# Gate products of a token stage as three-part fp32r products, with the parts made by GpSimd, ScalarE and VectorE

## What is computed

```python
out_swa = _swa(x_in, wq, wk, wv, wo)                # windowed attention
upd = ...                                           # one gradient step on a two-layer MLP (w1, b1, w2, b2)
out_mem = _mlp(*upd, k_flat)                        # silu(x @ w1.T + b1) @ w2.T + b2 with the updated weights
g1 = jax.nn.sigmoid(out_swa @ lin1.T)
g2 = jax.nn.sigmoid(out_mem @ lin2.T)
out_merged = g1 * out_swa + g2 * out_mem
...
x = x + ga * out_merged
h = _layernorm(x) * (1 + cb) + sb                   # input of router, shared expert and routed experts
```

## Time and profile before

| | |
|---|---|
| median of three runs | 1879.82 us |
| profiled execution | 1880.22 us, its span 1878.5 us |
| TensorE busy | 1827.2 us (97%) |
| VectorE, ScalarE, GpSimd busy | 1230.8, 955.1, 946.2 us |
| stage 2, 755 to 1213 us: TensorE, VectorE, ScalarE, GpSimd busy | 452.6, 327.1, 217.8, 248.4 of 458 us |
| granted TensorE clock in each stage | 0.99 |

### The profile page before, as it was taken

The page is one execution under the profiler, slowest core; times in us unless marked ns, Lnnn a source line. Parts: engine busy times, 40 slices in busy tenths (PEclk is TensorE's granted clock), DMA queues, the critical chain, the costliest instruction groups (busy, mean ns, idle before and its releaser), DMA issues.

```text
span 1878.5 us, 36384 instructions
## 1 busy us (share of the span) xinstructions
PE 1827.2 (97%) x12428; PEld 1607.6 (86%) x12428; DVE 1230.8 (66%) x2454; ACT 955.1 (51%) x1789; POOL 946.2 (50%) x667
## 2 busy tenths in 40 slices
PE   7999999999999999999999999998999999999995
PEld 5888888888888888677788877898999999999994
DVE  8877777777777777566776668744555555555552
ACT  6656666666666665545453354333344444444341
POOL 5666566666666665025666656644323333323234
PEclk9999999999999999999999999999999999999998
DMA  6211111111111100302111012267889888898883
GB/s 228 68 38 38 34 34 37 34 35 36 37 34 46 43 31 21 130 20 69 46 47 46 16 30 63 69 207 233 289 280 289 290 286 263 289 290 285 285 281 85
DMA packets 141016, 234.08 MB, mean 125 GB/s; under 512 B 24756, under 2 KB 88971, under 8 KB 140816
## 3 DMA queue, kind: packets, MB, share of 16 engines
q1 hardware_dynamic: 116368, 220.50, 34.3%
q0 software_dynamic: 24576, 12.69, 4.6%
HBM read 194.58 MB, written 78.45 MB: 145 GB/s over the span
## 4 chain that ended last, share of the span: by engine, by line
PE 53%; DMA 3%; issue 2%; POOL 1%; DVE 1%; SPq 0%; ACT 0%; POOLq 0%; DVEq 0%; ACTq 0%
PE bank L85 26%; PE bank L1904 21%; PE bank L1169 4%; DMA out_rows<-c_y_rest,c_token_rest 2%; DMA c_w<-in_e1T 1%; PE bank L2126 1%; POOL out_rows L2078 1%; PE bank L1668 1%; POOL slots L1863 0%; DMA slots<-last_row,last_index 0%; PE bank L2137 0%; DVE b_h_low L1450 0%; SPq L1960 0%; DVE early L1547 0%; DVE c_y_rest L2045 0%
## 5 line engine op out<-in xcount | busy, mean ns | idle before, releaser
L1904 PE MATMUL bank<-c_xT,c_w 128*128 128x160 f32 x3072 | 431.1, 300 | 5.7 <-DMA c_w<-in_e1T 5.0
L1904 PEld LDWEIGHTS bank<-c_xT,c_w 128*128 128x128 f32 x3072 | 420.5, 190 | 7.1 <-DMA c_w<-in_e1T 6.0
L1863 POOL DMA_INDIRECT slots<-b_row,b_index x224 | 249.1, 1112 | 199.1 <-issue 117.9
L2078 POOL DMA_INDIRECT out_rows<-c_y,c_x x64 | 100.2, 1565 | 374.0 <-DMA out_rows<-c_y_rest,c_token_rest 220.2
L2026 DVE TENSOR_TENSOR c_gT<-bank,c_sil 128x480 f32<-128x480 f32 x128 | 84.2, 658 | 218.8 <-PE bank L1904 209.8
L1994 ACT CAST c_gTs_high<-c_gT 128x384 fp32r<-128x384 f32 x128 | 65.6, 513 | 137.5 <-DVE c_gT L2026 121.2
L1987 ACT ACTIVATE c_sil<-bank 128x480 f32<-128x480 f32 x128 | 73.0, 570 | 113.0 <-PE bank L1904 100.9
L2019 DVE TENSOR_TENSOR c_gTs_low<-c_gT,c_gTs_high 128x384 fp32r<-128x384 f32 x128 | 71.7, 560 | 74.6 <-ACT c_gTs_high L1994 64.1
L456 POOL TENSOR_TENSOR last_row<-last_row,a_e 128x256 f32<-128x256 f32 x33 | 54.4, 1649 | 125.7 <-DVE a_e L712 124.1
L85 PE MATMUL bank<-c_w2s_high,c_gTs_high 128*128 128x256 f32 x384 | 114.2, 297 | 0.9 <-DVE c_gTs_low L2019 0.9
L85 PE MATMUL bank<-c_w2s_high,c_gTs_low 128*128 128x256 f32 x384 | 107.1, 279 | 0.0
(11 more groups left out here) (329 smaller groups left out, 5455.4 us busy)
## 6 DMA issues: line engine op xcount, KB each, us to landing
c_w<-in_e1T SPq DMA_DIRECT2D x64, 1536.0 KB
c_w<-in_e2T SPq DMA_DIRECT2D x48, 768.0 KB
early<-in_e2T SPq DMA_DIRECT2D x16, 768.0 KB
slots<-a_fill SPq DMA_DIRECT2D x16, 642.0 KB
c_x<-slots SPq DMA_DIRECT2D x64, 160.5 KB
a_x_in<-in_x SPq DMA_DIRECT2D x32, 128.0 KB, 2.1
xT_tiles<-a_xT SPq DMA_DIRECT2D x32, 128.0 KB
swaT_tiles<-a_swaT SPq DMA_DIRECT2D x32, 128.0 KB
```

The costliest lines, as they stand in the source:

```text
L1863: pool.indirect_dma_start(out=T["slots"], out_offset=bass.IndirectOffsetOnAxis(ap=index[:, t, k:k + 1], axis=0), in_=row[:, t, :], in_offs ...
L1904: return nc.tensor.matmul(out, lhsT, rhs, start=first, stop=last, skip_group_check=True)
L2078: pool.indirect_dma_start(out=T["out"], out_offset=bass.IndirectOffsetOnAxis(ap=token, axis=0), in_=rows, in_offset=None, bounds_check=las ...
```

## The change

In stage 2 both gate products become split products. linT is held as two parts, linT_high and linT_low; it is loaded into the place of x2 as the first load of the stage, GpSimd rounds the high part and VectorE makes the low part. For each chunk GpSimd rounds swaT to high_swaT and subtracts to get low_swaT (`split_swaT`): for chunks 0 and 1 at the start of its program, for chunk c+1 at group k=4 of the scatters of `routed_chunk(c)`, before the pace wait of that group. For om, ScalarE rounds high_om (`om_high`, between the sigmoids of the two gates) and VectorE makes low_om right after each om block. TensorE waits for `swaT_low` and, by k, for `om_high` and `om_low`.

The new buffers take addresses of others: low_swaT that of om, high_swaT that of g1, high_om that of g2, low_om that of hm; `fits` is `rest`. So `split_swaT` waits for the turning of the merged rows (`mT_mm`), `om_high` waits for `mT_mm` and `base_out`, and the sigmoid of g1 waits for both gate products of attention.

```diff
-        sp.dma_start(linT[:], T["linT"]).then_inc(S("lin_in"), 16)
+        sp.dma_start(lin_raw, T["linT"].rearrange("p a k d -> p (a k d)")).then_inc(S("lin_in"), 16)
+        load_swaT(0)
         for cols, raw in s1_raw:
             sp.dma_start(raw, T["s1T"].rearrange("p k n -> p (k n)")[:, cols]).then_inc(S("s1_in"), 16)
...
+        def split_swaT(c):
+            wait_apart(pool, S("swaT_in"), 16 * (c + 1), S("passed_pool"))
+            if not isinstance(c, int) or c > 0:
+                wait_apart(pool, S("mT_mm"), 2 * c, S("passed_pool"))
+            pool.tensor_copy(flat(high_swaT[:]), flat(swaT[:])).then_inc(S("swaT_high"), 1)
+            wait_apart(pool, S("swaT_high"), c + 1, S("passed_pool"))
+            pool.tensor_tensor(flat(low_swaT[:]), flat(swaT[:]), flat(high_swaT[:]).bitcast(F32), ALU.subtract).then_inc(S("swaT_low"), 1)
+
         def pace(c, k):
+            if k == 4:
+                split_swaT(c + 1)
...
+        pool.wait_ge(S("lin_in"), 16)
+        pool.tensor_copy(flat(linT[0][:]), lin_raw).then_inc(S("lin_high"), 1)
+        split_swaT(0)
+        pool.wait_ge(S("s1_low"), len(s1_raw))
+        split_swaT(1)
         routed_chunk(1, 1, pace)
...
+        def om_high(c):
+            wait_past(act, S("mT_mm"), 2 * c)
+            wait_past(act, S("base_out"), (c - 1) * 16)
+            for m in range(DC):
+                act.wait_ge(S("om"), 2 * c + m + 1)
+                act.copy(block_of(high_om, m), block_of(om, m)).then_inc(S("om_high"), 1)
...
             for g, (dst, banks) in enumerate(((g1, (5, 6)), (g2, LIN2_BANK if after else LIN2_FIRST))):
+                if g == 1:
+                    om_high(c)
                 for m in range(DC):
-                    act.wait_ge(S("lin_mm"), c * 4 + 2 * g + m + 1)
+                    act.wait_ge(S("lin_mm"), c * 4 + 2 * g + (m + 1 if g else DC))
...
                    .then_inc(S("om"), 1)
+                dve.wait_ge(S("om_high"), 2 * c + m + 1)
+                low(block_of(low_om, m), block_of(om, m), block_of(high_om, m)).then_inc(S("om_low"), 1)
...
         clamps()
+        dve.wait_ge(S("lin_high"), 1)
+        low(flat(linT[1][:]), lin_raw, flat(linT[0][:])).then_inc(S("lin_low"), 1)
...
         def gate_of_attention(c, m):
             for k in range(DC):
-                ins = mm(bank(5 + m), linT[:, 0, k, m * P:(m + 1) * P], block_of(swaT, k), k == 0, k == DC - 1)
+                ins = mm_split(nc, bank(5 + m), cut(linT, slice(None), 0, k, slice(m * P, (m + 1) * P)),
+                               [block_of(a, k) for a in swaTs], k == 0, k == DC - 1)
...
+        def gate_of_memory(c, banks):
+            for k in range(DC):
+                pe.wait_ge(S("om_high"), 2 * c + k + 1)
+                for a, part in enumerate((0, 1)):
+                    for m in range(DC):
+                        mm(bank(banks[m]), linT[part][:, 1, k, m * P:(m + 1) * P], block_of(high_om, k),
+                           k == 0 and a == 0, False)
+                pe.wait_ge(S("om_low"), 2 * c + k + 1)
+                for m in range(DC):
+                    ins = mm(bank(banks[m]), linT[0][:, 1, k, m * P:(m + 1) * P], block_of(low_om, k),
+                             False, k == DC - 1)
...
-                pe.wait_ge(S("lin_in"), 16)
-            pe.wait_ge(S("swaT_in"), 16 * (c + 1))
+                pe.wait_ge(S("lin_low"), 1)
+            pe.wait_ge(S("swaT_low"), c + 1)
```

More of the change, by code:

```diff
@@ L1115, in token_stage @@
     w1T, w2T, mod, ident, b1c, b2c = (buf[k] for k in ("w1T", "w2T", "mod", "ident", "b1c", "b2c"))
-    linT = sb("linT", [P, 2, DC, D])
+    linT_high = sb("linT_high", [P, 2, DC, D], F32R)
     wgT = sb("wgT", [P, DC, E])
@@ L1132, in token_stage @@
     hidden = buf["early"][:].rearrange("p (j n) -> p j n", j=HC)
-    om = sb("om", [P, TPC, D])
-    g1 = sb("g1", [P, TPC, D])
-    g2 = sb("g2", [P, TPC, D])
+    with ExitStack() as plain:
+        om, g1, g2 = (plain.enter_context(nc.sbuf_tensor("b_" + name, [P, TPC, D], F32)) for name in ("om", "g1", "g2"))
+    low_swaT, high_swaT, high_om = (sb(name, [P, TPC, D], F32R) for name in ("low_swaT", "high_swaT", "high_om"))
     x = sb("x", [P, TPC, D])
     x2 = sb("x2", [P, TPC, D])
-    hm = sb("hm", [P, TPC, D])
+    with ExitStack() as plain:
+        hm = plain.enter_context(nc.sbuf_tensor("b_hm", [P, TPC, D], F32))
+    low_om = sb("low_om", [P, TPC, D], F32R)
     hT = sb("hT", [P, DC, CH])
@@ L1147, in token_stage @@
     rank = sb("rank", [P, TPC, E])
-    fits = sb("fits", [P, TPC, E])
+    fits = rest
     slot = sb("slot", [P, TPC, E])
@@ L1163, in token_stage @@
     row = [sb(f"row{p}", [P, TPC, ROW]) for p in range(2)]
+    sb("low_shift", [P, SHIFT // 12])
+    linT = (linT_high, sb("linT_low", [P, 2, DC, D], F32R))
+    lin_raw = x2[:].rearrange("p t d -> p (t d)")
+    swaTs, oms = (high_swaT, low_swaT), (high_om, low_om)
     def bank(b, n=CH):
@@ L1234, in store @@
             sp.dma_start(out_rows[:, tiles(c - 1), :], base[:]).then_inc(S("base_out"), 16)
+        sp.dma_start(lin_raw, T["linT"].rearrange("p a k d -> p (a k d)")).then_inc(S("lin_in"), 16)
+        load_swaT(0)
         for cols, raw in s1_raw:
             sp.dma_start(raw, T["s1T"].rearrange("p k n -> p (k n)")[:, cols]).then_inc(S("s1_in"), 16)
-        load_swaT(0)
-        sp.dma_start(linT[:], T["linT"]).then_inc(S("lin_in"), 16)
         sp.dma_start(wgT[:], T["wgT"]).then_inc(S("wg_in"), 16)
@@ L1299, in gpsimd @@
         last_slot = pool.to_reg(E * CAP - 1)
-        pool.wait_ge(S("s1_low"), len(s1_raw))
+        pool.wait_ge(S("lin_in"), 16)
+        pool.tensor_copy(flat(linT[0][:]), lin_raw).then_inc(S("lin_high"), 1)
         def routed_chunk(c, p, step):
@@ L1390, in body @@
             for g, (dst, banks) in enumerate(((g1, (5, 6)), (g2, LIN2_BANK if after else LIN2_FIRST))):
+                if g == 1:
+                    om_high(c)
                 for m in range(DC):
-                    act.wait_ge(S("lin_mm"), c * 4 + 2 * g + m + 1)
-                    wait_past(act, S("mT_mm"), 2 * c)
-                    if g == 1:
-                        wait_past(act, S("base_out"), (c - 1) * 16)
+                    act.wait_ge(S("lin_mm"), c * 4 + 2 * g + (m + 1 if g else DC))
                     act.activation(block_of(dst, m), by_tile(bank(banks[m])), ACT.Sigmoid)\
@@ L1762, in gate_of_attention @@
             for k in range(DC):
-                ins = mm(bank(5 + m), linT[:, 0, k, m * P:(m + 1) * P], block_of(swaT, k), k == 0, k == DC - 1)
+                ins = mm_split(nc, bank(5 + m), cut(linT, slice(None), 0, k, slice(m * P, (m + 1) * P)),
+                               [block_of(a, k) for a in swaTs], k == 0, k == DC - 1)
             ins.then_inc(S("lin_mm"), 1)
+        def gate_of_memory(c, banks):
[9 more added lines that the diff above has]
+                             False, k == DC - 1)
+                    if k == DC - 1:
+                        ins.then_inc(S("lin_mm"), 1)
         def hidden_layer(c, after, js):
@@ L1806, in body @@
                 ranks(c)
-            for k in range(DC):
-                pe.wait_ge(S("om"), 2 * c + k + 1)
-                for m in range(DC):
-                    ins = mm(bank((LIN2_BANK if after else LIN2_FIRST)[m]), linT[:, 1, k, m * P:(m + 1) * P], block_of(om, k), k == 0, k == DC - 1)
-                    if k == DC - 1:
-                        ins.then_inc(S("lin_mm"), 1)
+            gate_of_memory(c, LIN2_BANK if after else LIN2_FIRST)
             if after and not last:
```

## The result

The changed kernel takes 1908.13 us (median of 6 runs, 1898.06 to 1913.91), the kernel before, beside it, 1880.28 (1879.34 to 1886.24). The ratio is 1.014, with a 95% interval of 1.0116 to 1.0164: slower, as predicted, but by 28 us at the medians where +7.6 was predicted, and outside the range of 1882.0 to 1892.5. The profiled execution is the shortest of the six: 1898.06 us, with a span of 1896.3 against 1878.5 before. So the trace can account for 17.8 us of the difference, and not for the 28 us between the medians.

What follows compares the result with a forecast made beforehand. TensorE was taken as the bound, only 0.88 us ahead of the hm chain; -0.5 us up to the end of chunk 1 and +8.1 for six chunks gave +7.6, so 1887.4 us, range 1882.0 to 1892.5.

Steps and rivals of the forecast that it cites:

- The hold: Chunks 2 to 7: GpSimd's copy and subtraction of swaT block VectorE's 128x4 inverse-root steps, delaying hm by 3.2 us.
- rivals 1 and 2: Inverse-root steps in stage 2: 1, no hold reaches them, -10.4 us, chance 0.14; 2, only the subtraction holds, +2.8 us, 0.08.
- rival 3: GpSimd's swaT copy takes its upper bound of 1.75 us: hm delayed 3.9 us, +11.8 us in all, chance 0.10.
- rival 4: Main case plus the om chain 0.4 us late in each chunk: +3.2 us, 1890.6 us, chance 0.06.
- The sum: Each of six chunk boundaries: hm turned 2.38 us later, 1.035 gained after it, +1.35 us a chunk, +8.1 in all.
- Chunks 0 and 1: Start of stage 2 to the end of chunk 1: gain less a shorter hold at boundary 0 to 1, -0.5 us.
- The gain of 1.1 in chunk 0: Chunk 0's four gate product pairs, less the om wait, bring its last gate product and merge about 1.1 us earlier.
- The om side: Memory gate in each chunk: om's high and low parts arrive just in time, cost zero, at most 0.4 us a chunk.
- Stage 3 "shifts as a whole": Stage 3 starts by TensorE's end of stage 2 and moves with it, adding no gain or loss.

Runs made afterwards that it cites:

- experiment 7: Changed kernel with GpSimd's copy and subtraction of swaT one scatter earlier (k=3, not k=4): median 1882.86 us, ratio 1.0017 to the kernel before.
- experiment 5: Changed kernel with TensorE computing one attention gate product twice more where it waited for hm: median 1892.89 us, ratio 1.0075 to the kernel before.
- experiment 2: Kernel before, fp32 products kept, plus GpSimd's rounding copy and subtraction into dead buffers at k=4 of six chunks: median 1904.67 us, ratio 1.014.
- experiment 12: Kernel before with three more 128x1024 subtractions on VectorE ahead of the inverse root at six boundaries: median 1910.66 us, ratio 1.0159.
- experiment 1: The changed kernel run again, nothing altered: median 1904.99 us, ratio 1.0163 to the kernel before.
- experiment 3: Changed kernel with only the memory rows' (om) gate split; attention gate fp32, no GpSimd pair: median 1883.27 us, ratio 1.0023 to the kernel before.
- 11: Only the memory rows' gate split, and in the last chunk the slots' index computed behind the merge: median 1885.92 us, ratio 1.0029 to the kernel before.
- experiment 4: Changed kernel with only the attention rows' (swaT) gate split, GpSimd's pair kept, memory gate fp32: median 1911.13 us, ratio 1.017 to the kernel before.
- 8: Changed kernel with swaT's high part made by ScalarE and low part by VectorE, GpSimd keeping chunk 0's: median 1874.77 us, ratio 0.9978 to the kernel before.
- 9: Kernel with swaT's parts made by ScalarE and VectorE, plus the last chunk's slots' index behind the merge: median 1876.84 us, ratio 0.9975 to the kernel before.
- experiment 10: Kernel with swaT's parts made by ScalarE and VectorE, run again without alteration: median 1876.59 us, ratio 0.9985 to the kernel before.
- experiment 6: Changed kernel with both attention gate products ahead of the turn of hm, not one: median 1899.18 us, ratio 1.0116 to the kernel before.

## Why the prediction was right in direction and wrong in size

**The hold: right.** The chief step of the prediction, that VectorE's short steps stand still under GpSimd's two instructions, is what the trace shows, and rivals 1 and 2 fall with it; rival 3 falls with the copy's 1.06 us, rival 4 with the om side. The copy took 1.06 us (estimate 1.05), the subtraction 2.39. The copy starts at +6.42 and not at +7.0, so that it holds the first 128x4 step and the subtraction the third, but the two held steps still make 3.2 us together, as forecast. The delay of hm is 3.5 us, and its turn at +16.17 in place of +15.90, because of something else: the prediction said that the change moves GpSimd's scatters of k=4 behind the chain, and they run beside its end, where L1624 takes 1.64 us for 1.40. That is 0.3 us a chunk too little in the sum; that the scatters cause it is read from the times and not tested. The Trainium skill's page "SBUF — State Buffer", section "SBUF: two separate sides", puts the hold as an exclusive lock on a shared port pair for the whole instruction; the 1.20 and 2.34 us of the two held steps agree. It limits the lock on VectorE's side to operations in a two-port mode or with two inputs in SBUF; the one-input statistics of experiment 7, unheld at 1.41 us, agree with that.

**The sum: the failed step.** "hm is then ready at 12.64 + 3.2 = 15.84, and TensorE turns it at 15.90 in place of 13.52: +2.38. After that come swaT m=1 and the two om pairs: -1.035." Everything behind the wait was priced at full clock, and the sum has no term for what the wait does to it. TensorE runs at half for some 3.4 us instead, which costs 1.7 us by the stretches of 2 us, 1.5 by experiment 5 (idle time filled), 1.5 to 1.9 by the chunks with and without a fall in experiment 2; experiment 12 shows that it needs neither GpSimd's pair nor the split products. With it a chunk comes to 1.35 + 0.3 + 1.7 = 3.35 us; measured are 3.4 (16.95 / 5). I had a wait of 2 to 3 us in the forecast and no row of the kernel before with such a wait in the loop; I bounded the copy, the om chain and the start, but not what a wait does to the clock. The Trainium skill's page "TensorE: Matmul & The Clock Gate", section "HAM oscillation — how this bites in real kernels", describes a like case: a stall that recurs in each tile makes TensorE pay for the way back to full clock in each. Its stalls are waits for DMA and longer than the 2.84 to 2.87 us here. The trace agrees, with 1.7 us after five of the six waits, and differs in that the sixth was free.

**Chunks 0 and 1: wrong by 1.15 us.** The forecast was -0.5, the trace has +0.65. The gain of 1.1 in chunk 0 did not come: g is turned at 790.35 against 790.17. Two things ate it. In this execution TensorE reached its first gate product 0.92 us later than before (769.95 against 769.03); in experiment 1 it was 1.26 us earlier (767.77), so this part is spread between executions. And the om products, 0.69 us shorter in themselves, brought nothing: those of k=1 start 0.27 us late (785.22), when ScalarE has made their high part, and both sigmoids of g2 now start behind the last product, so that the second ends 4.22 us behind the first om product, where it was 4.23. In chunk 1 the first step of the inverse root took 1.49 us (at 796.42), a hold of 1.3 where 1.6 was forecast, and hm is turned 13.75 us behind g, where it was 12.43. The clock's fall at 792 to 797 us is hidden under that: experiment 1, without it, has 13.74.

**The om side: zero, right in the loop, wrong in chunk 0 and in the last chunk.** In the loop the profile lists no wait for om, and by experiment 3 at most 0.1 us a chunk is missing (0.6 gained of 0.69). But in the last chunk, where the fp32 products of om had covered VectorE's slot work, TensorE now waits 1.20 us for g. I had asked what is late next at six boundaries, and not at the last turn of g, where the order of the work is another. With 0.3 for the later turn of hm this makes 1.5 of the 1.86 us between the last chunk's +3.21 and the forecast +1.35.

**Stage 3 "shifts as a whole": wrong by -3.0 us here,** and by +6.8 and +9.2 us in experiments 3 and 11 (a lead of 3.1 and of 5.4 us at the last turn of g, and 3.7 and 3.8 us behind at the end). Here it happened to bring the time nearer to the forecast.

**Together,** in the profiled execution: forecast +7.6; clock 5 x 1.7 = 8.5; the later turn of hm 6 x 0.3 = 1.8; chunks 0 and 1 1.15; last wait 1.2; stage 3 -3.0. This gives 17.3 of the 17.8 us (the terms are rounded, and the last chunk keeps 0.4 unexplained).

**What stays open.** The medians differ by 28 us, the profiled executions by 18. The number and length of the clock's falls vary between executions (five of six and six of six in two profiles of the same kernel; 10.3 and 15.4 us lost in the changed kernel and in experiment 4), which could make such a spread. That is argued: no trace of one of the longer executions was taken. The mean granted clock is on record for every execution, and supports it in part. It is 0.983 and 0.982 in the executions of 1913.9 us against 0.986 and 0.987 in the two of 1898, which by (1 - clock) x span is an estimate of 7 to 9 of the 16 us; in the one of 1912.5 us it is 0.986, and the clock explains next to nothing.

## What to carry to other kernels

Price a wait of the bounding engine twice: by its length and by what TensorE's clock does behind it; in this kernel a wait of 2.8 us cost 4.5 where a fall followed. Before an idle GpSimd is given a 128x1024 operation, look at what VectorE does in those microseconds: one place earlier, where they ran beside the norm's statistics, the same instructions cost a fraction, and on ScalarE and VectorE they turned the loss of 1.4% into a gain of 0.15 to 0.25% (experiments 8, 9 and 10; one of the three intervals reaches 1). And where a split or a faster operation takes work off the bound, ask at every boundary, the last one included, which chain had been hidden by it.

## What the hardware showed that I had not expected

- The granted clock fell to the 1.2 GHz level behind waits of 2.5 to 2.9 us (five and six of six in two executions of the changed kernel, four of six in experiment 2, six of six in 4), behind three of six of 2.85 to 3.17 (experiment 12), twice in six behind 1.5 plus 0.73 us (experiment 6), and never behind the single waits of 0.7 to 1.6 us in experiment 7. There is no sharp rule in the length of a wait. Behind the same two waits of 0.75 and 1.27 us at the end of chunk 0 it fell in one execution of a program and not in another: in the changed kernel and not in experiment 1, in experiment 10 and not in 8.
- A fall mostly cost 1.7 us, that is 3.4 us at half clock, and about 3.4 us where it lasted twice as long (once or more in each of experiments 3, 4, 6, 7 and 9 to 12).
- A fall does not show as idle time. TensorE's busy time was 1826.2 us against 1827.2, with 11 us less work in it; only the clock column tells.
- Adding 2.7 us of useless products a chunk made a kernel 5 to 7 us faster in its trace and 12 us at the median.
- GpSimd's one-input copy of 128x1024 ran in 1.06 us (1.38 and 1.80 where it began while VectorE's 128x1024 add still ran), its two-input subtraction in 2.39 to 2.41 (3.15 once, in experiment 4), ScalarE's copy of the same size in 1.05, and VectorE's subtraction in 1.24.
